# VectorE reads a batch's ranks from PSUM instead of from ScalarE's 16-bit copy, in the second half of a sorting loop

## The reference, cut to what matters

```python
xn = _layernorm(x)
# graph layer: two sparse products over the edges, row=src, col=dst
low  = relu(segment_sum(edge_weight[:, None]    * (xn @ weight_low )[dst], src, 6250))
high = relu(segment_sum(edge_weight_n2[:, None] * (xn @ weight_high)[dst], src, 6250))
mlp  = relu(xn @ weight_mlp)
gnn  = 3 * (att[:, 0:1] * low + att[:, 1:2] * high + att[:, 2:3] * mlp)   # att: softmax of logits
# mixing layer: q, k, v = xn @ w_qkv; k and v normalised; kv = k.T v over all nodes; q @ kv; a GELU MLP
x = x + gnn + mix(xn)
x = x + ffn(_layernorm(x))        # the half of the nodes with the largest weights goes through an MLP
```

## Time and profile before

| what | us |
|---|---|
| median of 3 runs | 2471.05 (2466.08 to 2477.81) |
| the profiled execution | 2489.27 |
| its span, first to last instruction | 2487.5 |
| busy in the span: PE, DVE, ACT, POOL | 1724.4, 1253.1, 895.6, 1376.2 |
| pick 14, the first that the change touches, starts at | 422.52 |
| pick 27 starts at | 743.68 |
| the last of the 448 scatters ends at | 806.01 |
| the first gather starts at | 822.81 |

### The profile page before, as it was taken

The page is one execution under the profiler, slowest core; times in us unless marked ns, Lnnn a source line. Parts: engine busy times, 40 slices in busy tenths (PEclk is TensorE's granted clock), DMA queues, the critical chain, the costliest instruction groups (busy, mean ns, idle before and its releaser), DMA issues.

```text
span 2487.5 us, 30925 instructions
## 1 busy us (share of the span) xinstructions
PE 1724.4 (69%) x9081; PEld 1439.1 (58%) x9081; DVE 1253.1 (50%) x3123; ACT 895.6 (36%) x2606; POOL 1376.2 (55%) x1351
## 2 busy tenths in 40 slices
PE   4788886998845257775776777777677577577672
PEld 3566665787734146665665566666566466456562
DVE  8899986899752133333333332333333333333336
ACT  2667664787643022222222222222222222222223
POOL 3377774777776554545556455455455555555600
PEclk9899986999967668987888888888788788788886
DMA  3121101111100532323223223222222222222203
GB/s 90 46 54 38 48 13 36 38 55 54 38 5 5 126 80 69 79 68 78 70 69 84 68 73 74 67 73 72 66 75 73 72 72 76 77 70 69 85 9 103
DMA packets 206265, 156.60 MB, mean 63 GB/s; under 512 B 143354, under 2 KB 177676, under 8 KB 206092
## 3 DMA queue, kind: packets, MB, share of 16 engines
q0 software_dynamic: 55232, 113.59, 16.3%
q1 hardware_dynamic: 150860, 40.90, 7.4%
HBM read 139.76 MB, written 14.64 MB: 62 GB/s over the span
## 4 chain that ended last, share of the span: by engine, by line
PE 48%; issue 25%; ACT 8%; DVE 8%; POOL 7%; another core or an unknown queue 4%; DMA 1%; SPq 0%; DVEq 0%; ACTq 0%; POOLq 0%
PE bank L1514 46%; POOL sorted_records L647 6%; ACT arena L1308 1%; ACT base L1308 1%; ACT side L1308 1%; PE bank L1789 1%; POOL arena L664 1%; ACT arena L1429 1%; ACT side L1505 1%; DVE arena L807 1%; ACT arena L1433 1%; ACT arena L1312 1%; DVE arena L732 0%; ACT base L1354 0%
## 5 line engine op out<-in xcount | busy, mean ns | idle before, releaser
L1514 PE MATMUL bank<-arena 128*128 128x128 f32 (+3 forms) x6320 | 1305.4, 360 | 524.0 <-issue 434.5
L1514 PEld LDWEIGHTS bank<-arena 128*128 128x128 f32 (+1 forms) x6320 | 1098.1, 205 | 710.9 <-issue 547.5
L664 POOL DMA_INDIRECT arena<-xn_rows,arena x852 | 830.1, 974 | 740.5 <-SPq L558 460.5
L647 POOL DMA_INDIRECT sorted_records<-arena x448 | 522.3, 1166 | 249.5 <-issue 142.4
L1172 DVE CUSTOM_DVE_ANT_0 arena<-arena 128x256 f32<-128x256 f32 x98 | 37.8, 422 | 399.9 <-ACT arena L1438 363.1
L1177 DVE SCALAR_TENSOR_TENSOR att_prod<-sg,att_neg 128x9 f32<-128x9 f32 x49 | 8.5, 173 | 361.3 <-issue 319.6
L1124 DVE TENSOR_TENSOR arena<-arena 128x640 f32<-128x640 bf16 (+1 forms) x204 | 164.0, 804 | 41.9 <-DVE arena L1118 14.0
L1118 DVE SCALAR_TENSOR_TENSOR arena<-io,arena 128x320 bf16<-128x320 f32 (+1 forms) x204 | 97.7, 479 | 146.7 <-issue 65.4
L1476 ACT ACTIVATE arena<-bank 128x256 f32<-128x256 f32 x49 | 18.8, 383 | 401.5 <-remote 278.9
L1514 PE MATMUL bank<-arena,base 128*128 128x128 f32 (+3 forms) x766 | 119.8, 290 | 17.3 <-ACT base L1312 8.9
L807 DVE TENSOR_TENSOR arena<-arena 128x1280 f32<-128x1280 bf16 x84 | 120.6, 1488 | 18.7 <-remote 17.8
(11 more groups left out here) (306 smaller groups left out, 1875.5 us busy)
## 6 DMA issues: line engine op xcount, KB each, us to landing
arena<-xn_rows,arena POOLq DMA_INDIRECT x852
arena<-in_x SPq DMA_DIRECT2D x24, 512.0 KB
sorted_records<-arena POOLq DMA_INDIRECT x448
xn_rows<-arena SPq DMA_DIRECT2D x12, 512.0 KB
arena<-xn_rows SPq DMA_DIRECT2D x12, 512.0 KB
out<-base SPq DMA_DIRECT2D x4, 1024.0 KB
arena<-in_L_ffn_w SPq DMA_DIRECT2D x2, 1024.0 KB, 6.3
arena<-sorted_records SPq DMA_DIRECT2D x54, 32.0 KB
```

What stands on the lines that cost most here:

```text
L647: pool.indirect_dma_start(rec_dram, bass.IndirectOffsetOnAxis(ap=idx[0:PR, par, u:u + 1], axis=0), stage_rec[0:PR, par, u * 8:(u + 1) * 8] ...
L664: pool.indirect_dma_start(gring[:, c % GR, :], None, xn_dram, bass.IndirectOffsetOnAxis(ap=rring[:, c, 3:4].bitcast(I32), axis=0)).then_in ...
L1514: return pe.matmul(out_, lhsT, rhs, start=start, stop=stop, **kw)
```

## The change

From batch 14 on, `pick_rank` waits for `rank_ready` and reads `bank[0]` itself, in 32 bits. ScalarE's `copy_rank` runs for batches 0 to 13 only; the 14 copies of batches 14 to 27 are gone. As VectorE is now the reader of the bank, `chunk_dests(g)` waits for `prod_set`, the end of the pick, where it waited for the copy; this begins with `chunk_dests(13)`.

```diff
             def pick_rank(g):
 
-                dve.wait_ge(S("rank_copied"), g + 1)
+                if g < MIX:
+                    dve.wait_ge(S("rank_copied"), g + 1)
+                    rank = rankf[:, :]
+                else:
+                    dve.wait_ge(S("rank_ready"), g + 1)
+                    rank = bank[0][:, 0:RANKS]
                 dve.tensor_tensor(prod4[:, :, :, 0:NB], oh[:, :, :].rearrange("p (s j) b -> p s j b", s=GROUPS),
-                                  rankf[:, :].rearrange("p (s b) -> p s b", s=GROUPS).unsqueeze(2).to_broadcast([P, GROUPS, GS, NB]),
+                                  rank.rearrange("p (s b) -> p s b", s=GROUPS).unsqueeze(2).to_broadcast([P, GROUPS, GS, NB]),
                                   ALU.mult).then_inc(S("prod_set"), 1)
...
-                if more:
+                if g + 1 < MIX:
                     copy_rank(g + 1)
...
             def chunk_dests(g):
 
                 pe.wait_ge(S("steps_set"), g + 1)
-                pe.wait_ge(S("rank_copied"), min(g + 2, G) if g else 1)
+                if g + 1 < MIX:
+                    pe.wait_ge(S("rank_copied"), g + 2 if g else 1)
+                else:
+                    pe.wait_ge(S("prod_set"), min(g + 2, G))
```

## The result

| | kernel before | changed kernel |
|---|---|---|
| median, us | 2470.55 (20 runs, 2457.22 to 2488.34) | 2507.26 (20 runs, 2472.07 to 2545.94) |
| profiled execution: span, us | 2487.5 | 2520.7 |
| last scatter of the sort ends at | 806.0 | 854.0 |
| first gather starts at | 822.8 | 870.6 |

The ratio is 1.0071, 95% interval 1.0048 to 1.0093: slower, where no change was forecast (2468 us, range to 2481). The ratio leaves out executions more than 1.5% above a kernel's fastest, and ten of the changed kernel's 20 are; the medians are 1.5% apart. The changed kernel on two more chips gave 1.0159 (1.0104 to 1.0213) and 1.0258 (1.0200 to 1.0317).

A forecast was written before the change was run, and what follows sets the result against it. It took GpSimd's scatters to set the pace from pick 22 on, but TensorE's slow stretches to set the sort's end; reaching them 2.7 us earlier, kept as -3, gave a median of 2468 us, range 2455 to 2481.

The forecast's parts named there:

- The pick at 3.2 us: VectorE's pick: 3.2 us from the slope between two 32-bit rows, +1.5 us for each of 14; bounds 1.69 and 3.91.
- The copy and its wait are worth nothing by themselves: ScalarE loses 5.8 us of copies and a 1.51 us wait; worth nothing, as ScalarE isn't the bound.
- Tight slots of 22.7 us: Slots where VectorE's own work sets the period: 21.43 - 0.2 + 1.5 = 22.7 us.
- GpSimd no longer held: Scatters under picks 15 to 24 lose 8.4 us of holds; last scatter of batch 24 ends 6.3 us earlier.
- 4.0 us that the prediction counts as held: GpSimd, batches 15 to 24: 24.2 us each against 20.2 at full pace, so 4.0 us in held-up scatters.
- TensorE's slow stretches: End of the sort, 684 to 784 us: length unchanged, tied to TensorE's program; reached with pick 25, 2.7 us earlier.
- Slow stretches of another length: Sign that the forecast is wrong: TensorE's slow stretches changing length, which would outweigh all other terms.
- shorter: Full-gain rival: stretches follow GpSimd or shrink when it is less busy; 6 to 17 us gained, about 2459 us; 21%.
- at a fixed time: No-effect rival: stretches sit at a time, or the end waits for the dense layers; 2471 us, plus or minus 3; 20%.
- The new wait costs nothing: `chunk_dests` waiting for the pick: cover of 4 us in the slot of pick 18, so no cost.
- The sum of -3 us: Whole kernel: -2.7 us at the end of the sort, kept as -3 with the clock; 2468 us median.
- slower: Rival: the new pick holds GpSimd too, +1.5 us for each of picks 15 to 24, 15 us; 2486 us; 14%.
- Part 1: The pick gets slower, +1.5 us each; by the skill's copy-first advice alone 14 picks would cost 21 us.

The follow-up runs named there:

- f1: Changed kernel, but VectorE first copies the ranks from PSUM to 16 bits in SBUF and picks from that copy; ratio 1.0049.
- a0: The changed kernel run again unaltered, in another job; ratio 1.0159, last scatter at 849.5 us.
- i1: Kernel before with picks from PSUM from batch 14 on, and GpSimd waiting for a pick ahead of a batch's fifth scatter; ratio 0.9976, chip at 0.93.
- e1: Kernel before with only TensorE's wait ahead of the destinations changed: for the pick, not ScalarE's copy; ratio 1.0011.
- e3: Kernel before, but from batch 14 on ScalarE's copy is 32-bit in SBUF and the pick reads that; ratio 1.0080.
- f2: Kernel before with ScalarE's waits and copies kept; from batch 14 on the pick reads PSUM, destinations wait for copy and pick; ratio 1.0254.
- h1: Kernel before with picks of batches 0 to 13 reading PSUM and later ones the 16-bit SBUF copy, all copies kept; ratio 1.0259.
- f3: Changed kernel in which TensorE's first permutation matmuls of a batch also wait until the next batch's pick is over; ratio of medians 1.036.
- g3: Kernel before; from batch 14 on VectorE first does the pick from PSUM (overwritten), then the 16-bit pick from SBUF; ratio 1.0065.
- j2: Picks from PSUM from batch 14 on, GpSimd waiting for a pick ahead of a batch's fifth scatter, on a chip at 0.83; ratio 1.0096.
- i3: Kernel before with the pick reading PSUM only from batch 21 on; ratio 0.9972 on a chip at 0.93.

## Why the prediction was wrong, point by point

1. **The pick at 3.2 us**: right, 3.217. The slope between two rows was the good estimate, line 890 scaled (3.91) the bad one.
2. **The copy and its wait are worth nothing by themselves**: right as far as f1 shows; a free ScalarE with a 16-bit pick gains nothing (1.0049).
3. **Tight slots of 22.7 us**: the term is right where TensorE keeps time: 22.4 us between these two picks of a0, and 22.8 us in i1 (where the pick still waits for ScalarE).

```profile
618.45 3.21 DVE L770 TENSOR_TENSOR arena<-arena,bank 128x2940 f16<-128x2940 bf16 x1
...
640.88 3.21 DVE L770 TENSOR_TENSOR arena<-arena,bank 128x2940 f16<-128x2940 bf16 x1
```

   In the changed kernel's profile hardly any slot is so: they take 27 to 33 us, as VectorE waits for TensorE.
4. **GpSimd no longer held**: right, 37 scatters of 37, and worth nothing here, since GpSimd now waits for VectorE's line 830 (11 times from 414 us on, 76.2 us in all), which waits for TensorE. The 4.0 us that the prediction counts as held in each batch contain a gap of 3.3 us inside batch 21 that isn't a hold, 0.3 us a batch. On the chip at 0.93 the freed scatters may be what makes 0.997, but no run there isolates them.
5. **TensorE's slow stretches**: this step failed. "I take them as tied to their place in TensorE's program, with their length unchanged." They are tied to no place, and their length is not a constant. Three executions of the changed program have 7, 10 and 10 of ten slots with one, and the kernel before has 2, in slots that e1 and e3, with picks from SBUF, run clean. In the changed kernel's ten slots the third permutation ends 15.5 to 20.6 us behind the ranks, in those of the kernel before 7.6 to 11.1 us. The profile of before had the warning in it: three stretches of 15, 27 and 16 us that no wait of the program explains, more than all other terms together, and I carried them as a constant into a sum of 3 us. The same kind of pause fills the part behind the sort (294 of them), where the prediction didn't look. Slow stretches of another length were listed as what would make the forecast wrong, but the rivals had them shorter, or at a fixed time, and in none did they grow, so the range ended at 2481.
6. **The new wait costs nothing**: right, e1 is at 1.0011.

The sum of -3 us was thus made of good terms and one unknown, and with it the end of the sort moved by 48 us in the profiled execution. Of the rivals "slower" had the right side for a wrong reason: the pick doesn't hold GpSimd. Part 1 also weighed the advice of the Trainium skill ("VectorE: DVE Perf Modes", "Rules for kernel authors") to copy from PSUM to SBUF first where many operations follow, and priced it at 1.5 us a pick. That advice is right for this kernel on a chip at 0.83, and by more than VectorE's own time: f1 follows it and is 2% faster than f2 on the same chip.

**What stays open.** Shown is: with only the operand in PSUM (f2) TensorE's results come late in most slots, with a pick of the same length from SBUF (e3) they don't, and the effect goes where such picks go (h1). It comes on chips with a mean granted clock near 0.83 and not on the one near 0.93, and only the first have TensorE's pauses in steps of 0.70 us. Not shown is what makes these pauses, and how a pick from PSUM brings them on. f3 and i1 exclude a plain collision at PSUM; and g3, the same read with a 16-bit pick behind it, contradicts a simple "reading PSUM does it". One rival is left untested: that the pauses answer to how much TensorE and the other engines have just done, and not to the read as such. For it are the slots of f3 in which TensorE had rested and the first five picks of h1. Kernels with all picks from SBUF have such slots now and then (before 2 of 10, f1 2), so the read makes more frequent what is there anyway. Whether the change itself is faster on a chip at 0.93 wasn't measured.

None of the versions beats the kernel before on a chip at 0.83; the nearest is e1, the same within 0.4%.

## What to carry to other kernels

An engine's idle time marked "issue", with results that arrive later than its rows end, is a term of its own: if it is larger than the gain you sum up, the forecast must carry it as a rival with the range that its size gives, not as a constant. Compare a row that ends with the row of the one that reads its result; a gap of 6 us there tells of a slowed engine before the starts break up. Look for such pauses in the whole trace, not only where the change lies. And measure a change on more than one chip: the kernel of i1 and j2, with picks from PSUM, is 0.2% faster than the one before on one kind and 1.0% slower on the other.

## What the runs showed of the hardware

- **Two kinds of chip.** The kernel before takes 2467 to 2483 us on four chips and 1990 us on a fifth. From 845 us on the granted TensorE clock is 0.82 on the first kind (the kernel before) and 0.98 on the second (i3).
- **On the slower kind TensorE pauses in steps of 0.70 us.** The 16 traces have 292 to 419 such pauses marked "issue" behind 441 us, the four of the faster chip none.
- **TensorE can lag behind its rows.** A permutation with a row that ends at 508.76 us raised its semaphore at 512.34, and transposes with one that ends at 511.43 were read at 517.45. The granted clock was at its full level until 517.0 us and at 1.2 GHz only from there to 523.8.
- **VectorE's operand in PSUM can cost more than its own time.** The 3.22 us pick has the same length from 32-bit SBUF and from PSUM. With the first, scatters that start under it are held (14 of 14) and no slot is disturbed (e3). With the second they pass (30 of 30) and 8 of 10 slots are disturbed, at 0.83 (f2).
- **The cost doesn't follow the length of the read** (at 0.83, on three chips): a third of it, 1.18 us, gives 1.0195, the whole 1.0254, twice of it 1.0392, and the whole ahead of a 16-bit pick 1.0065.
